# Self-attention: the value products of the last key tile stand between the two pairs of score and maxima products instead of behind both

## The reference, cut to what matters

```
def _mha(x, ctx, mask, qw, qb, kw, kb, vw, vb):
    q = _split_heads(x @ qw + qb)
    k = _split_heads(ctx @ kw + kb)
    v = _split_heads(ctx @ vw + vb)
    scores = jnp.einsum('bqhd,bkhd->bhqk', q, k) / np.sqrt(D // H).astype(np.float32)
    ...
    probs = jax.nn.softmax(scores, axis=-1)
    out = jnp.einsum('bhqk,bkhd->bqhd', probs, v)
    return out.reshape(x.shape[0], x.shape[1], D)
sa = _mha(x, x, None, sq_w, sq_b, sk_w, sk_b, sv_w, sv_b)
```

## Time and profile before

| | us |
|---|---|
| three runs | 1152.61, 1158.29, 1154.33 |
| median | 1154.33 |
| profiled execution, device time | 1152.13 |
| its span, first to last instruction | 1150.0 |
| PE busy in the span | 1041.5 |
| DVE busy | 787.9 |
| ACT busy | 612.1 |
| POOL busy | 329.4 |

### The profile page before, as it was taken

One profiled execution on the slowest core, in us unless ns is written; L12 is line 12 of the kernel. 1 busy time (PEld: TensorE's weight loads), 2 busy tenths in 40 slices (PEclk: granted clock), 3 DMA queues, 4 the chain that ended last, 5 costly groups with the idle time before them and its releaser, 6 DMA issues.

```text
span 1150.0 us, 20772 instructions
## 1 busy us (share of the span) xinstructions
PE 1041.5 (91%) x7648; PEld 610.4 (53%) x7648; DVE 787.9 (69%) x1337; ACT 612.1 (53%) x1191; POOL 329.4 (29%) x724
## 2 busy tenths in 40 slices
PE   5699789988999999999996998949899999999997
PEld 3366456633333333333334556635787776576765
DVE  1567547676999999999954268443745677887575
ACT  2266346435888888888883221302222355656543
POOL 3211211101312312312312334272375644521010
PEclk8799989976999999999999999878999999999999
DMA  7402210260221221221215110010144411100000
GB/s 192 74 6 97 91 48 16 92 224 13 69 75 47 72 72 49 68 73 49 68 37 183 60 37 19 1 72 21 60 164 142 127 52 38 38 29 1 20 14 23
DMA packets 97730, 75.67 MB, mean 66 GB/s; under 512 B 49875, under 2 KB 87648, under 8 KB 97376
## 3 DMA queue, kind: packets, MB, share of 16 engines
q1 hardware_dynamic: 94559, 65.96, 19.4%
q0 software_dynamic: 3072, 8.39, 2.2%
HBM read 42.94 MB, written 30.93 MB: 64 GB/s over the span
## 4 chain that ended last, share of the span: by engine, by line
PE 69%; DVE 11%; DMA 6%; ACT 5%; issue 4%; SPq 4%; POOL 2%; DVEq 0%; ACTq 0%; POOLq 0%
PE TR L800 16%; PE OUT L800 14%; PE OUT L995 10%; PE TR L806 9%; PE TR L984 8%; DMA head_q<-MT 4%; PE OUT L984 4%; PE TR L910 2%; PE SCR L894 2%; ACT PTS L1235 2%; DVE small L1427 2%; PE SCR L887 1%; SPq L689 1%; PE OUT L806 1%; POOL dispatched L1917 1%
## 5 line engine op out<-in xcount | busy, mean ns | idle before, releaser
L1535 DVE TENSOR_REDUCE small<-SCR 128x1 f32<-128x1024 f32 x256 | 308.4, 1224 | 27.6 <-PE SCR L968 21.5
L1297 ACT ACTIVATE shared<-TR 128x512 f32<-128x512 f32 x351 | 199.6, 597 | 34.5 <-PE TR L984 23.1
L968 PE MATMUL SCR<-head_k,head_q 48*128 48x512 f32 x512 | 200.7, 470 | 3.6 <-DVE small L1535 1.7
L995 PE MATMUL OUT<-shared,HM 128*32 128x256 f32 x2048 | 166.1, 396 | 1.3 <-ACT shared L1297 0.4
L984 PE MATMUL TR<-head_q,head_k 51*128 51x512 f32 x351 | 146.7, 455 | 7.1 <-issue 3.6
L1801 POOL TENSOR_SCALAR small<-small 128x1 f32<-128x1 f32 x112 | 27.5, 246 | 393.9 <-DVE small L1428 391.8
L800 PE MATMUL TR<-xT,fifo 128*128 128x512 f32 x224 | 111.2, 656 | 2.8 <-ACT xT L1215 2.8
L1297 ACT ACTIVATE shared<-OUT 128x512 f32<-128x512 f32 x161 | 96.4, 599 | 27.3 <-PE OUT L984 27.2
L984 PEld LDWEIGHTS TR<-head_q,head_k 51*128 51x128 f32 x351 | 61.0, 187 | 78.1 <-ACT shared L1297 43.1
L1215 ACT ACTIVATE xT<-TR 128x256 f32<-128x256 f32 x96 | 35.6, 381 | 113.2 <-PE TR L806 112.6
L995 PEld LDWEIGHTS OUT<-shared,HM 128*32 128x32 f32 x2048 | 41.4, 108 | 94.0 <-ACT shared L1297 56.7
(11 more groups left out here) (242 smaller groups left out, 1876.6 us busy)
## 6 DMA issues: line engine op xcount, KB each, us to landing
pieces<-pieces SPq DMA_DIRECT2D x16, 512.0 KB, 2.8
HM<-dispatched SPq DMA_DIRECT2D x46, 128.0 KB
expert_out<-HM SPq DMA_DIRECT2D x46, 128.0 KB
dispatched<-HB SPq DMA_DIRECT2D x6, 768.0 KB, 4.0
head_q<-pieces SPq DMA_DIRECT2D x32, 128.0 KB
head_k<-pieces SPq DMA_DIRECT2D x32, 128.0 KB
shared<-in_L_ffn_w SPq DMA_DIRECT2D x4, 1024.0 KB, 11.7
X<-in_x SPq DMA_DIRECT2D x1, 2048.0 KB, 9.6
```

The source lines that it names most:

```text
L968: ins = nc.tensor.matmul(SQ[kt % 2][:, hf, :], QX[n % 2][rows, kt * 128:(kt + 1) * 128], KX[n % 2][rows, hf * 512:(hf + 1) * 512], start=T ...
L995: ins = nc.tensor.matmul(PV[32 * g:32 * g + 32, 0:256], VH[:, n % 2, kt, :], PTB[:, kt % 2, g * 256:(g + 1) * 256], start=(kt == 0), stop= ...
L1297: nc.scalar.activation(PTB[:, kt % 2, hf * 512:(hf + 1) * 512], ring_bank("t_scores", n, kt, hf), ACT.Exp, scale=DH ** -0.5).then_inc(st_d ...
L1535: nc.vector.tensor_reduce(nm[:, n % 2, kt:kt + 1], SQ[kt % 2].rearrange("p h n -> p (h n)"), AX, ALU.max, negate=True).then_inc(sq_done.se ...
```

## The change

`values` for the last key tile is issued between the two pairs of score and maxima products (behind that of the first half, hf = 0) instead of behind both. The count of exps for which it waits is written with 1 instead of 2, because one `t_scores` fewer has been issued by then: it names the same exp, that of the second half of the key tile that `values` works on. No instruction is added or removed. The last `values` of the whole part, behind the loop, stays where it was.

```
                         t_scores(tl, n, kt, hf)
                         if n + 2 < NH:
                             max_scores(tl, n + 2, kt, hf)
-                    if kt > 0:
-                        values(tl, n, kt - 1, 2)
-                    elif n > 0:
-                        values(tl, n - 1, QT_PER_HEAD - 1, 2)
+                        if hf == 0 and kt > 0:
+                            values(tl, n, kt - 1, 1)
+                        elif hf == 0 and n > 0:
+                            values(tl, n - 1, QT_PER_HEAD - 1, 1)
                     if kt == 3 and n + 1 < NH:
                         maxima_transpose(n + 1)
                     if kt == 5 and n >= 1:
                         head_out_transposes(n - 1)
```

## The result

The changed kernel takes 1477.26 us (median of 4 runs, 1476.67 to 1479.9) against 1153.47 us (1149.77 to 1158.29) before on the same chip: ratio 1.2808, 95% interval 1.2757 to 1.2859. The prediction of 1487 us is 10 us, 0.7%, too high.

What follows compares the result with a forecast made beforehand. TensorE and VectorE were taken as level at 1.23 us a key tile. At half clock 255 x 2.49 + 31 x 1.32 = 676 us, 332 more than 344.4, plus 3 behind, gave 1487 us; range 1258 to 1508.

Steps and rivals of the forecast that it cites:

- an exp in series with each interval: Part b: pair, exp, value products in series, 1.75 us a key tile at full clock, 2.49 at half, against 1.23.
- The clock: Part b starts at half clock, and the clock likely does not rise there; stage 676 us against 344.4.
- the mixed case: Rival: the clock comes and goes in part b; 1378 us with half at each level, chance 0.08.
- The support that the prediction took from b0: Gaps under a microsecond in part b0 were said to have been enough to lose the full clock at 244 us.
- the half clock throughout: Likeliest case: all of part b runs at half clock, 1487 us in all, chance 0.66.
- The rule of the Trainium skill: By it gaps of 0.33 to 0.52 us would not matter; the full-clock rival, about 1270 us, chance 0.22.
- (c): Once a head, the transpose of maxima between two pairs: hidden at full clock, +0.33 us at half.
- (b): Once a head, the transposes of line 806 between two pairs: +0.09 us at full clock, +0.70 at half.
- (a): A head's first value products also wait for `head_output`, behind the exp on ScalarE: +0.29 us.
- The 3 us for the part behind: The part after part b would start at half clock instead of full, adding 3 us.
- The wait for the DMAs: At a head's start, waiting for the maxima's DMAs, 14.8 us for 25 heads, would be gone; no separate term.
- not slower: Rival: the exp is done within two pairs' 0.66 us; intervals stay 1.23, 1152 us, at best 10 less; chance 0.02.

Runs made afterwards that it cites:

- 1: Changed kernel with the changed order from head 4 on only, heads 0 to 3 keeping the order of before; 1401.94 us.
- 5: Changed kernel with filler matmuls behind each pair of maxima products in part b0 and 12 more at its end; 1393.66 us.
- 2: Changed kernel with each exp, after the first two key tiles, taken of 256 of its 512 columns; 1439.67 us.
- 9: Changed kernel with value products of the key tile two before, a third exp buffer, and `head_output` behind key tile 1's first exp; 1190.99 us, ratio 1.0353.
- Experiment 8: Changed order in heads 0 to 15, the order of before in heads 16 to 31; 1331.32 us.
- 7: Changed kernel with filler matmuls in part b0 and also in front of the value products of most key tiles; 1329.08 us.
- 4: Changed kernel with one filler matmul in front of the value products of seven key tiles in eight; 1680.67 us.
- experiment 12: Kernel before with `maxima_transpose` and `maxima_rows` at key tile 2 instead of 3, so their DMAs are requested earlier; 1152.21 us, ratio 0.9998.

## Why the prediction was right

**The core, an exp in series with each interval: shown.** The rows of after have the chain link by link (0.83, 0.60, 0.05, 1.01), the full-clock length came out at 1.76 against 1.75 for a plain key tile, and at 1.79 against 1.80 with what comes once in a head (experiments 1 and 5), a shorter exp shortens the interval one for one (2), and a longer lead takes the wait away (9).

**The clock: right, and its reason partly shown.** That it does not rise in part b is in the trace of after. Experiment 8 shows that the order decides it, and 7, by one execution, that filled gaps keep it up. But "the gaps keep it from rising" is too simple: in 4 the gaps were filled at half clock and it didn't rise either. And the mixed case, which I gave 0.08, is what the order does when it starts at full clock (1 and 5): it holds for 94 or 190 us. What ends it at 400.7 and at 456.8 us, no row shows; that stays open. Of the loss, 255 x 1.785 - 344.4 = 111 us are what the order costs at full clock, nearly all of it the exp wait, and the other 214 us are the clock.

The support that the prediction took from b0 was weak, and to that extent the half clock throughout was luck. It says that gaps under a microsecond lost the clock there. The trace has TensorE idle for 1.39 us in front of the first maxima product (240.91) and 0.93 in front of the one at 243.00, and busy for 1.88 of the last 4 us before the fall. The changed order at full clock is busy for 74.56 of 93.70 us with no idle time above 0.8 us, a much denser pattern, and it held the clock for 94 us before losing it.

**The rule of the Trainium skill** (TensorE: Matmul & The Clock Gate, the table on why this matters), by which idle gaps below some 3 us cost no clock, would have given 1270 us. Measured were 1477, with 700 us at half clock. The one idle time of TensorE above 3 us in them is 3.6 us in front of part b's first pair (265.44), with the clock at half already; behind it none is above 0.8 us until the clock rises at 943. In experiments 1 and 5 it fell with none above 0.8 us either, since 307 us in the one and 266 us in the other. The measurement decides against the rule here.

**The sum, term by term.** These are median intervals between the first weight loads of successive groups of value products, heads 8 to 27, in us:

| interval | before | after | predicted |
|---|---|---|---|
| four or five plain ones | 1.23 to 1.26 | 2.49 to 2.52 | 2.49 |
| with the maxima transpose, (c) | 1.44 | 2.67 | 2.49 + 0.33 |
| with the transposes of L806, (b) | 1.60 | 3.08 | 2.49 + 0.70 |
| with `head_output`, (a) | 1.30 | 2.78 | 2.49 + 0.29 |
| whole head | 10.61 | 21.02 | 21.24 |

(The kernel before has 1.33 in one interval more.) The plain interval and (a) are exact. (b) and (c) were too high, 0.59 for 0.70 and 0.18 for 0.33. Their single pairs are as I had them, 0.72 us (614.20 to 614.92). The transposes are shorter: twice the full-clock 0.37 was 0.74 for the two of L806, and they take 0.62 (614.92 to 615.54); half of that was 0.37 for the transpose of maxima, and it takes 0.21 (609.77 to 609.98). The whole head is 0.22 us shorter than predicted, 7 us over 31 heads.

**The 3 us for the part behind: not there.** It takes 538 us against 539, though its first 7 us are at half clock now. These 3 and the 7 above are the 10 us by which the prediction was high.

**The wait for the DMAs was mis-sized and put down to the wrong transfer** (experiment 12). Of the 0.6 us a head, 0.41 are the idle time that stands before such a pair anyway, and 0.18 are a wait. The prediction needed no term for it, because the stage was counted whole, and the wait is gone in the changed kernel as it says. But the 10 us that the rival "not slower" would have gained are 5 or 6 at most.

**What the prediction had not seen** is that the value products' place between the halves holds the maxima buffers longer. By the reading of 9 it is 36.5 us when nothing covers it, and none here. The rival "not slower" missed it: with the exp in time the kernel takes 1191 us, not 1152.

No version was faster than the kernel before beyond its interval.

## What to carry to other kernels

Where an in-order engine alternates with another, count how many independent instructions stand between a producer and its consumer, and compare their time with the whole latency (here 0.53 + 0.60 + 0.05 us against two pairs of 0.66), not with the other engine's busy share, which was 42% here. Then look at what the new gap does to the clock, because this was worth twice the gap itself. A name beside a wait tells what ended last, and not why it ended so late: experiment 12 moved the request by a key tile, and the landing stayed where it was.

## What the runs showed of the hardware

- The clock that was granted to one order of work differed by the clock with which it began: at 1.79 us a key tile it ran for 94 us and for 190 us at full clock and then fell to half for the 456 and 396 us that were left of the part, while started at half it never left it. These are single executions, four for the last. TensorE's idle time before L995 at full clock was 0.8 us at a time.
- At half clock, products that fill 97% of TensorE's time did not raise it in 895 us (experiment 4); the same fillers under a full clock kept it for 500 us (7).
- ScalarE's exps of 0.60 us start 0.49 us apart when they are ready: 612.54 and 613.03 above.
- Three small transfers (4 KB each) landed 3.2 us after the first of them was asked for when the queue had nothing before them, and 5.0 and 6.3 us after it behind 384 KB of the same queue, each time with the end of those (experiment 12).
